# Pairs of heads in layer one's convolution, odd heads placed by a transfer, running sums in place of averages

## What is computed

```python
avg = cumsum(h, axis=tokens) / (1, 2, ..., 1024)      # running mean over tokens, per head: v
pe  = v @ W_pe + b_pe                                  # 16 -> 2 * 31
e   = pe[..., :31] * sigmoid(pe[..., 31:]) + stt_energy
w   = softmax(e, axis=taps)                            # 31 weights for each token and head
out = sum over taps k of w[t, head, k] * v[t - 30 + k, head]   # the convolution
out = layernorm(out @ W_fc + h) * gamma + beta
```

## Time and profile before

| | |
|---|---|
| median of three runs | 3462.36 us |
| the profiled execution | 3466.14 us, its span 3464.3 us |
| TensorE busy, share of the span | 3307.4 us, 95% |
| VectorE | 2606.8 us, 75% |
| ScalarE | 2076.2 us, 60% |
| GpSimd | 1269.7 us, 37% |
| mean granted TensorE clock | 0.979 |

### The profile page before, as it was taken

One profiled execution on the slowest core, in us unless ns is written; L12 is line 12 of the kernel. 1 busy time (PEld: TensorE's weight loads), 2 busy tenths in 40 slices (PEclk: granted clock), 3 DMA queues, 4 the chain that ended last, 5 costly groups with the idle time before them and its releaser, 6 DMA issues.

```text
span 3464.3 us, 67597 instructions
## 1 busy us (share of the span) xinstructions
PE 3307.4 (95%) x25168; PEld 2785.4 (80%) x25168; DVE 2606.8 (75%) x6172; ACT 2076.2 (60%) x4055; POOL 1269.7 (37%) x1073
## 2 busy tenths in 40 slices
PE   7999999999996999999999469999999999999999
PEld 4888888888885799999999347888888888888888
DVE  5877887788777865555554578888888888888884
ACT  4677777777765555655665345555555555555554
POOL 1333333332331366666665332333333332322320
PEclk8999999999998999999999689999999999999999
DMA  5332233222212344444444465555655555655541
GB/s 180 102 114 90 93 114 108 80 64 80 75 45 80 87 115 103 96 104 109 105 97 86 86 132 113 113 127 127 129 125 127 120 123 126 130 125 128 128 102 41
DMA packets 746021, 366.38 MB, mean 106 GB/s; under 512 B 551278, under 2 KB 696246, under 8 KB 745558
## 3 DMA queue, kind: packets, MB, share of 16 engines
q1 hardware_dynamic: 717278, 319.57, 36.4%
q0 software_dynamic: 28416, 42.49, 6.6%
HBM read 224.93 MB, written 135.99 MB: 104 GB/s over the span
## 4 chain that ended last, share of the span: by engine, by line
PE 87%; DVE 6%; ACT 2%; DMA 2%; issue 1%; SPq 1%; POOL 1%; POOLq 0%; DVEq 0%; ACTq 0%
PE bank L2294 10%; PE bank L853 10%; PE bank L1612 10%; PE bank L2308 10%; PE bank L1596 10%; PE bank L833 10%; PE bank L2265 7%; PE bank L130 5%; PE bank L810 3%; PE bank L2244 3%; PE bank L2276 3%; PE bank L2239 1%; ACT sides L1140 1%; PE bank L818 1%; PE bank L846 1%
## 5 line engine op out<-in xcount | busy, mean ns | idle before, releaser
L1492 DVE TENSOR_TENSOR hidden_low<-bank,hidden_high 128x512 fp32r<-128x512 f32 x256 | 176.2, 689 | 263.0 <-ACT hidden_high L1193 262.8
L609 ACT ACTIVATE bank<-bank,b 128x512 f32<-128x512 f32 x256 | 172.7, 675 | 282.2 <-PE bank L833 281.9
L1186 ACT ACTIVATE bank<-bank,fc_bias 128x512 f32<-128x512 f32 x256 | 169.5, 662 | 263.5 <-PE bank L1596 263.5
L853 PE MATMUL bank<-w_high,gT_low 128*128 128x256 f32 x1024 | 309.8, 303 | 2.9 <-DVE gT_low L725 2.9
L2052 ACT ACTIVATE bank<-bank,l_b 128x512 f32<-128x512 f32 x256 | 168.9, 660 | 238.8 <-PE bank L2294 238.8
L2308 PE MATMUL bank<-l_w_high,l_hidden_low 128*128 128x256 f32 x1024 | 307.6, 300 | 0.0
L2265 PE MATMUL bank<-bandT,window 128*32 128x96 f32 x5632 | 271.2, 345 | 22.4 <-DMA bandT<-bands 20.2
L853 PE MATMUL bank<-w_low,gT_high 128*128 128x256 f32 x1024 | 289.4, 283 | 0.0
L853 PE MATMUL bank<-w_high,gT_high 128*128 128x256 f32 x1024 | 289.4, 283 | 0.0
L2308 PE MATMUL bank<-l_w_low,l_hidden_high 128*128 128x256 f32 x1024 | 286.0, 279 | 0.0
L2308 PE MATMUL bank<-l_w_high,l_hidden_high 128*128 128x256 f32 x1024 | 285.5, 279 | 0.0
(11 more groups left out here) (372 smaller groups left out, 10709.3 us busy)
## 6 DMA issues: line engine op xcount, KB each, us to landing
bandT<-bands SPq DMA_DIRECT2D x352, 240.0 KB, 3.7
fc_full<-in_L_ffn_fc_wT SPq DMA_DIRECT2D x32, 1024.0 KB, 5.5
bands<-zeros SPq DMA_DIRECT2D x22, 768.0 KB, 8.6
x<-in_L_attn_x SPq DMA_DIRECT2D x32, 512.0 KB, 6.3
moe_output<-zeros SPq DMA_DIRECT2D x32, 512.0 KB, 7.1
x_after_retention<-x SPq DMA_DIRECT2D x32, 512.0 KB, 2.9
moe_input_and_gates<-xn SPq DMA_DIRECT2D x32, 512.0 KB, 7.7
moe<-moe_output SPq DMA_DIRECT2D x32, 512.0 KB, 7.4
```

Source lines behind the costliest of these rows:

```text
L609: e.activation(bank[:, :], bank[:, :], ACT.Gelu_apprx_tanh, bias=t.b1[:, f:f + 1]).then_inc(s("g_full"), 1)
L853: m = pe.matmul(out, x, w, start=False, stop=f == KF - 1 and j == 2 and c % 2 == 1)
L1492: v.tensor_tensor(t.hidden.low[:, n % SLICES, :], K.banks[t.bank["expand", i, f, 0]][:, :], t.hidden.high[:, n % SLICES, :], ALU.subtract) ...
```

## The change

**Convolution.** `window` has one block of 32 columns for each pair of heads, the two heads interleaved (row 2d of the result belongs to the even head, row 2d+1 to the odd one), and no zeros. One matmul takes both heads: its moving operand is bandT[:, :, first:first+2], 192 columns, of which each two neighbours lie side by side. 8 matmuls for a window in place of 16, each with start and stop. In the result, even rows are valid in the even columns, odd rows in the odd ones.

**Placing.** ScalarE copies the odd columns to a new tile `odd` (L2040 of the changed kernel), then the even columns to convT (L2043), and a DMA from ScalarE's own queue (step `place_odd`, L2048) writes the odd partitions of `odd` over those of convT. `mix` waits for that DMA, where it waited for the copy. The rows of W_fc are permuted on their way in.

**Running sums.** `average` becomes `run_sum`: the scan writes sumT and there is no multiply. The counts go into scales of ScalarE, one number for each partition (token): the tanh has 0.5/count, the exponential 1/count, the window copy 1/count. The bias product has the counts in place of ones as its stationary operand, and ScalarE multiplies stt_energy by the counts for each chunk (L2015) before GpSimd adds it.

```diff
@@ layer_one_scalar
             if n >= 2:
                 e.wait_ge(s("gated_energy"), n - 1)
-            e.activation(t.th[n % 2][:, :, :], kernel_view(K, t, b, ch, 1), ACT.Tanh, scale=0.5).then_inc(s("gate"), 1)
+            if n >= 2:
+                e.wait_ge(s("full_energy"), n - 1)
+            e.mul(t.scaled_energy[n % 2][:, :, :], t.energy[:, :, :], t.count[:, ch:ch + 1]).then_inc(K.later("scaled_energy")[0], 1)
+            e.activation(t.th[n % 2][:, :, :], kernel_view(K, t, b, ch, 1), ACT.Tanh, scale=t.half_count[:, ch:ch + 1]).then_inc(s("gate"), 1)
...
-            e.activation(t.e[n % 2][:, :, :], t.e[n % 2][:, :, :], ACT.Exp).then_inc(s("exp"), 1)
+            e.activation(t.e[n % 2][:, :, :], t.e[n % 2][:, :, :], ACT.Exp, scale=t.per_count[:, args[0]:args[0] + 1]).then_inc(s("exp"), 1)
...
-            e.copy(out, src).then_inc(s("window"), 1)
+            e.activation(t.window[n % 2][:, :, :].rearrange("p a (d q) -> p a q d", q=2),
+                   K.banks[t.bank["window_turn", b, *args, 0]][:, 0:D].rearrange("p (a q d) -> p a q d", q=2, d=t.HD), ACT.Copy, scale=t.per_window[:, args[0]:args[0] + 1]).then_inc(s("window"), 1)
...
+            e.copy(t.odd[n % 2][:, :, 0:size], heads[:, :, 0:size, 1])
             if before:
                 e.wait_ge(s("mixed"), before)
-            e.copy(t.convT[:, :, place:place + size],
-                   K.banks[t.bank["convolve", b, i, 0]][:, 0:KD * TT].rearrange("p (k t) -> p k t", k=KD)[:, :, 0:size]).then_inc(s("convT"), 1)
+            e.copy(t.convT[:, :, place:place + size], heads[:, :, 0:size, 0]).then_inc(s("conv_taken"), 1)
+        elif name == "place_odd":
+            (i,) = args
+            n, size, place = b * NT + i, min(TT, K.S - i * TT), i * TT % t.CIRCLE
+            e.wait_ge(s("conv_taken"), n + 1)
+            e.dma_start(t.convT[1::2, :, place:place + size], t.odd[n % 2][1::2, :, 0:size]).then_inc(K.later(f"odd_placed{n % 2}")[0], 16)
@@ layer_one_vector
-            v.tensor_tensor(t.avgT[b % 2][:, k, PAD + half * BANK:PAD + (half + 1) * BANK], sums, t.per_count[:, tokens], ALU.mult).then_inc(s("avgT"), 1)
@@ layer_one_tensor
-                for odd in range(2):
-                    for g in range(4):
-                        pair = 4 * k + g
-                        m = pe.matmul(bank[32 * g:32 * (g + 1), k * TT:(k + 1) * TT], t.window[n % 2][:, pair, odd, :],
-                                      t.bandT[n % 2][:, :, g // 2 * H // 2 + k * t.HR + g % 2 * 2 + odd], start=odd == 0, stop=odd == 1)
+                for g in range(4):
+                    first = g // 2 * H // 2 + k * t.HR + g % 2 * 2
+                    out = bank[32 * g:32 * (g + 1), 2 * k * TT:2 * (k + 1) * TT].rearrange("p (t q) -> p t q", q=2)
+                    m = pe.matmul(out, t.window[n % 2][:, 4 * k + g, :], t.bandT[n % 2][:, :, first:first + 2], start=True, stop=True)
...
-            pe.wait_ge(s("convT"), NT * b + -(-(ch + 1) * P // TT))
+            last = NT * b + -(-(ch + 1) * P // TT) - 1
+            for n in range(max(last - 1, 0), last + 1):
+                pe.wait_ge(*K.later(f"odd_placed{n % 2}", 16 * (n // 2 + 1)))
@@ PLACES_D (one line of it)
-    "mix": (19.06, 20.4, 21.9, 24.8, 26.2, 27.7, 30.6, 31.43), ...
+    "mix": (19.15, 20.61, 22.1, 24.89, 26.55, 27.9, 31.19, 32.35),
```

More of the change, by code:

```diff
@@ L1633 @@
 PLACES_D = {
[L1634 to L1641, removed]
@@ L1642 @@
-    "mix": (19.06, 20.4, 21.9, 24.8, 26.2, 27.7, 30.6, 31.43), "center_mid": (19, 20.4, 21.9, 24.8, 26.21, 27.7, 30.6, 32),
-    "root_mid": (24.98, 32.56), "residual_mid": (25.83, 32.44), "stats_x3": (26.59, 34.51), "root_x3": (27.13, 35.02), "norm_x3": (27.48, 35.68),
-    "turn_mid": (29.71, 36.62), "load_out_row": 35.09, "gain_out": (42.68, 50.91), "result": (45.63, 54.65),
+    "l1_split": 0.56, "l1_low": 1.09, "l1_contract": 2.58, "share": (2.65, 10.18), "load": (0.27, 7.36),
+    "join": (4.53, 13.36), "add_in": (5.06, 13.12), "stats_in": (7.02, 13.73), "root_in": (8.85, 14.8),
@@ L1746, in layer_one_tiles @@
     t.bandT = K.ring(ctx, "bandT", 2, [P, TT, H])
-    t.window = K.ring(ctx, "window", 2, [P, H // 2, 2, 2 * t.HD])
+    t.window = K.ring(ctx, "window", 2, [P, H // 2, 2 * t.HD])
+    t.odd = K.ring(ctx, "odd_heads", 2, [P, KD, TT])
     t.o = K.tile(ctx, "o", [P, HC, D])
@@ L2238, in layer_one_tensor @@
                 rows = slice(r * P // 2, (r + 1) * P // 2)
-                pe.matmul(pair[r][:, 0:4 * t.RW], t.ones[rows, :], t.pe_bias[rows, :, :, :, :].rearrange("o a j q k -> o (a j q k)"), start=True, stop=False)
+                pe.matmul(pair[r][:, 0:4 * t.RW], t.counts[rows, ch * P:(ch + 1) * P], t.pe_bias[rows, :, :, :, :].rearrange("o a j q k -> o (a j q k)"), start=True, stop=False)
             for j in range(KD):
@@ L2440 @@
     arrays["w_pe_blocks"] = arrays["w_pe_blocks"].reshape(P, -1)
-    arrays["per_count"] = (np.float32(1) / np.arange(1, S + 1, dtype=np.float32)).reshape(1, S)
+    arrays["counts"] = np.arange(1, S + 1, dtype=np.float32).reshape(1, S)
+    arrays["token_counts"] = columns(arrays["counts"])
+    arrays["per_count"] = columns(np.float32(1) / arrays["counts"])
+    taps, reach = 96, P - 96
+    tokens = taps * np.arange(-(-S // taps))[None, :] + p[:, None] - reach
+    arrays["per_window"] = np.where((tokens >= 0) & (tokens < S), np.float32(1) / np.clip(tokens + 1, 1, S).astype(np.float32), np.float32(1))
     nc = bacc.Bacc("TRN2", target_bir_lowering=False, num_devices=1)
```

139 lines of the change are left out of this document (80 added, 59 removed).

## The result

The changed kernel takes 3512.6 us, median of four runs (3509.4 to 3519.9), against 3461.6 for the kernel before in the same job: a ratio of 1.0149 [1.0131, 1.0168]. It is 51 us slower; the forecast was 57 faster, and 3512.6 lies outside the range. The profiled execution has a span of 3511.3 us.

A forecast was written before the change was run, and what follows sets the result against it. TensorE was taken as the bound, busy 89.52 of 90.00 us a batch. A batch changes by -7.2 + 2.0 + 1.0, over 14.6 batches -61 us; with +3.5 and +1.5 at the start, -56: 3405 us, range 3356 to 3498.

The forecast's parts named there:

- The stream: TensorE's convolution: side-by-side pairs stream 192 columns at 0.80 to 0.85 ns each, saving 0.66 us a convolution, 7.2 a batch.
- Rival C: TensorE's convolution: four tiles share a read limit, so pairs save nothing and the new waits add 40 us: 3500, chance 18%.
- the landing: Sign in the trace: the placing transfer of the odd heads lands at 2.5 to 3 us.
- the mixes' wait: Sign in the trace: TensorE's mix waits for the placing transfer, 1 to 3 us a batch.
- VectorE's wait for GpSimd: Sign in the trace: VectorE waits for GpSimd under 2 us a batch, where it waited 6.9.
- the batch: Sign in the trace: a steady batch of layer one takes 85 to 87 us, where it took 90.0.
- one of my signs of being wrong: The forecast is wrong if TensorE's largest wait is on ScalarE or VectorE.
- Rival D: Placing transfer: landing under load takes 4.4 us, mixes wait 9 us a batch against 7.2 saved: 3490, chance 8%.
- I charge 0.4 each, 2.0 a batch: TensorE's mixes: five of a batch's eight wait 0.4 us for the placing transfer, 2.0 a batch, bounds 0 and 9.5.
- It stays under TensorE's 82.8: VectorE: without the multiply and most waits for GpSimd it needs about 78 to 79 us a batch, below TensorE's 82.8.
- for engines that now all stand over 84% and wait for one another in fixed order I charge 1.0 more (0 to 3): Coupling of the engines in layer one's batches: 1.0 us more a batch, bounds 0 to 3.
- Rival B: ScalarE or VectorE eats most of the saving through slow copies and blocking transfers, 2.5 to 3 us a batch: 3445, chance 14%.

The follow-up runs named there:

- e13: The changed kernel with residual_mid moved to 26.62, ahead of the gating, and GpSimd's add_row moved to 9.2 and 17.0: ratio 1.0012.
- e8: The kernel before, in its old order with averages, plus the convolution by pairs and both copies, without the placing transfer: ratio 0.9936.
- e10: The kernel before, in its old order, with pairs, both copies and running sums with ScalarE's scales, without the placing transfer: ratio 0.9893.
- e7: The kernel before with residual_mid moved to 26.82 and 34.84, just behind a gating, and stats_x3 to 26.9 and 34.9: ratio 1.0186.
- e14: e13 without the placing transfer (odd heads left unplaced): ratio 0.9907.
- e4: The changed kernel without the placing transfer (odd heads unplaced, both copies remain): ratio 1.0026, 3475 us.
- e1: The kernel before with the changed kernel's order of steps and banks and none of its operations: ratio 1.0172, 3525.5 us.
- e15: e13 with GpSimd's join of the first half moved from 4.53 to 3.2: ratio 1.0036.
- e16: e15 with each mix 0.1 to 0.2 of a slot later on TensorE, VectorE's list unchanged: ratio 1.0138.
- e9: The changed kernel with only GpSimd's add_row moved, from 11.51 and 19.58 to 9.2 and 17.0: ratio 1.0043.

## Why the prediction was wrong

**Right.** The stream. Rounds of four 192-column matmuls are 0.163 to 0.165 us apart at full clock (0.19 from the first to the second), so 0.85 ns a column where it was 1.71; TensorE has 83 us less to do over the program. Rival C is out. The Trainium skill's rule (SBUF — State Buffer, "Specifications (TRN2)", cachelines) fits: twice as many hits a line, half the time a column; no run with other spacings tells it from other causes of the strided read. Of the signs I had named, the landing, the mixes' wait and VectorE's wait for GpSimd came in as said, the batch did not; and one of my signs of being wrong came true, since TensorE's largest single wait is for VectorE's l_hidden_low.

**Right in size.** The transfer: 2.7 us in the median from the start of its issue to its landing, where I took 2.8:

```profile
L2048 ACTq DMA_DIRECT2D convT<-odd_heads x94: 601/602/618, 2308.0 to 3096.9; - x94
...
DMA to landing us min/median/max: 1.9/2.7/6.5
```

Rival D is out as a rule, but not in the tail. Its issue holds ScalarE's queue for 0.60 us, not 0.43. ScalarE works 61.2 us a batch (65 forecast): the exponential 0.70 in place of 0.63, the tanh 0.66 in place of 0.58, so 0.08 for a scale that is a column, where I took 0.12. The two copies take 0.32 and 0.33, as priced. The window copy takes 0.49 in place of 0.38, with a column and with every second number written; no run parts the two.

**Mis-sized.** "I charge 0.4 each, 2.0 a batch", the term for the transfer's wait: the mixes wait 15.9 + 9.9 us in 800, 3.0 a batch, and in e13, where nothing else is in the way, 4.5 (39.9 in 800). Taking the transfer out gives 43 us in the kernel after and 36 in e13, 2.5 to 3 us a batch. With 29 us forecast for it, that is 7 to 14 us of the 108 between forecast and result.

**The step that failed** is the one on VectorE: "It stays under TensorE's 82.8", and with it "for engines that now all stand over 84% and wait for one another in fixed order I charge 1.0 more (0 to 3)". VectorE's busy time was to be 75.1 us a batch and is 78.7 (677.4 in 800), with 12.5 us of waits on top, so 91.3 of 93.0. Rival B, by which ScalarE or VectorE eats the saving, came nearest in kind (the issues block for longer than 0.43, the gates come late) and was 68 us too low. There are two errors in the step.

One: I took 78 to 79 us as VectorE's need, and did not ask which of its waits stay when TensorE has less to do. e8 and e10 have no transfer and no new order, and get 22 and 37 us of 97. In e8, with VectorE at 77.5 busy, 6.2 of waits for GpSimd and 3.0 for ScalarE, the chain runs through VectorE and a batch lasts 88.5, so of the 7.2 us of the saving some 1.5 count. In the kernel after the waits for GpSimd did fall below 2 us a batch, as forecast; waits for the tanh (34.1 us in 800), for the exponential (23.6) and for TensorE stand in their place.

Two: I read the new order for what stands between a wait and its releaser, and not for what runs beside it. Where GpSimd's next instruction is the addition that VectorE's gating releases, a VectorE instruction placed right behind the gating meets it (in e7 it is not the next, and they do not meet). In the kernel before, the l_hidden_low stands there, which isn't held; in the one after, the residual, which is. In 800 us before, 71 of L2141 take 968 ns in the mean and 675 in the median, 20.8 us too much; after, 69 of L2161 (897), 44 and 24 of L2196 (901 and 866, median 478) are 43 too much: 2.3 and 5.0 us a batch. The Trainium skill has the rule (SBUF — State Buffer, "SBUF: two separate sides"): a VectorE instruction with two SBUF inputs and a GpSimd instruction that reads SBUF exclude each other for the whole instruction. The traces agree as far as they go: held are L2196 and L2161 (up to 2.60 us), not those that read a PSUM bank and not the reductions. Held too is a small one with a single tensor input (L654, 128x4: 0.17 us in the median, up to 0.77). Not seen to hold anything are GpSimd's own 128x4 instructions: in layer one of the kernel before, L2141 starts 16 times while one of 1.0 us (l_root_mid) runs, and never takes over 0.68 us. The rule would have told me to look; the rows of before (L2141, 962 ns in the mean, 675 in the median) already had it.

**The balance**: forecast -57, of which the saving was -105, with 15 charged for coupling, 29 for the transfer and 5 for the start. Measured in pairs of kernels: +47 for the two placements of residual and row addition (after against e13), +36 for the transfer (e13 against e14), -32 for all the rest (e14), in which TensorE, with 3.7 us a batch of waits, most of them for VectorE's l_hidden_low (17.7 in 800) and ScalarE's window copy (11.5), does not get its -105; together 51. The parts depend on the order in which they are taken: e4 against after gives 43 for the transfer, and e1's 58 for the new places is in a kernel in which TensorE has its old work. Not settled is what else in the new places costs; after both repairs e14 and e10, with the same operations in new and in old places, differ by 0.14%, within their intervals, so little can be left there; with the transfer in place no such pair was measured.

One slip is in the chances: C and D have 26% together, and slower was given 23.

## What to carry to other kernels

An engine at 87% is the next bound at once, not after the first has lost 7 us, if its waits are for answers to its own work (here 6.9 us a batch for the addition that its gating releases, and 6.2 still in e8): such waits stayed when the first engine had less to do. Add them to its busy time, and take a saving only down to that sum. The sum is a guide and no proof, since busy time and all waits nearly fill the batch of any engine; the chain of a run says which engine it is. When an order changes, look on VectorE not only at who waits for whom but at what GpSimd is running then: compare min, median and max of each line, since a median that stays and a maximum five times as long was here the mark of a hold. A step that is moved away from one collision has to be followed to the next (e15), and an added wait moved off one engine comes back on the engine behind it (e16).

## What was not expected of the hardware

The hold (up to 2.60 us on an instruction of 0.48, until GpSimd's instruction is over, and e9 shows that moving GpSimd's instruction alone ends the longest of it). And TensorE's clock, which falls inside the steady part. In the kernel after TensorE is busy for 1.56 of 4 us, and in the next 4 the granted clock is 0.69, a mean over its two levels, 1.2 and 2.4 GHz; in the steady batch before it was 1.00 throughout.

```profile
2368.00:2372.00 4.00, 1.56 (x8) 1.11 (x7) 3.96 (x5) 1.87 (x5) 2.13 (x1) 0.88 0.48 139
2372.00:2376.00 4.00, 4.00 (x33) 3.29 (x36) 2.63 (x6) 2.17 (x5) 0.00 (x0) 0.69 0.19 25
```

There are six such falls in the 800 us, where the kernel before has none, and ahead of each TensorE stood still for 1.7 to 3.0 of 4 us. Not every gap is followed by one: from 2741 to 2745 TensorE is busy for 1.57 us as well, and the clock stays at 1.00. The two of the five batches with a granted clock of 1.00 took 91.5 and 91.7 us, the three with 0.96 to 0.98 took 93.6 to 94.4; whether the falls made them longer or their gaps made both is not shown.
